# Where a running maximum's matmuls stand beside an attention tile's two score pairs, and where the matmuls of a key difference stand behind its values' matmul

## The chip, the cores and the metric

One NeuronCore of a Trainium2 chip runs the whole program, in one launch. The metric is the device time of one execution in microseconds. Of the kernel before three executions were timed; a fourth was taken with the hardware profiler.

## The reference

Four transformer layers work on x, 1024 tokens by 128. In each, x is increased by a cross-attention over 6404 context rows (16 heads of 8), and then by a mixture of 8 experts of which each token uses 2. Layers 0, 1 and 3 use a softmax, layer 2 a sigmoid. Cut to what matters here:

```
for l in 0..3:
    q = split_heads(norm(x) @ Wq.T + bq)         # 16 heads, 1024 x 8 each
    k, v = split_heads(ctx @ Wk.T + bk), split_heads(ctx @ Wv.T + bv)   # 6404 x 8 each
    s = q @ k.T / sqrt(8)                         # 16 x 1024 x 6404
    a = softmax(s) if l != 2 else sigmoid(s)
    x = x + (a @ v, heads joined) @ Wo.T + bo
    x = x + experts_l(norm(x))                    # top 2 of 8, gated (l = 2: gelu)
```

The softmax needs, for each query and head, a number near the largest score, so that no exponential overflows. The change concerns when those largest scores are found.

## The kernel before, in words

**Tiles and phases.** Tokens are taken in two blocks of 512 queries, so layer and block give 8 units; heads are taken in groups of 4, so there are 32 phases (4 per unit; `phase`, L122). A phase goes over 51 tiles of 128 keys. A tile has two score pairs: pair 0 is heads 0 and 1 of the group, pair 1 heads 2 and 3. Each pair is two matmuls of 32 x 128 against 32 x 512 in f16 (L787) into one half of the PSUM tensor `scores`, and one exponential of 128 x 1024 on ScalarE (L956). The four heads stand on four groups of 32 rows of TensorE: heads 0 and 1 ("half 0") on rows 0 to 63, heads 2 and 3 ("half 1") on rows 64 to 127. The values' matmul `av` (L797, eight matmul records of fp32) for the tile before follows behind pair 1.

**Maxima.** While phase p runs, the maxima of phase p+1 are prepared: 176 matmuls per phase (L818), each 128 queries of one head against 512 keys, into one of three banks of the PSUM tensor `side`; VectorE reduces each (L1070). 144 are plain. For the first 2048 keys a saving is made: two chunks are combined, since max(a, b) = b + relu(a - b). The stacks of differences of keys lie in `K` beside the keys; a `dif` step (L809) multiplies a pair of heads by such a difference into a half of `scores`, ScalarE takes the relu into the SBUF tile `above` (L964), and two combined maxima (L1074) add the second chunk's scores to it and reduce. There are 16 differences and 32 combined maxima per phase. `above` is single: a relu waits for both combined maxima of the difference before it.

**Waits.** `scores` has two halves, used in turn by score pairs, differences and some of the feed-forward matmuls (`in_pairs`, L166): a user waits until the one two before it has been read. `side` has three banks, used by maxima, transposes, `oT`, `flipmax`, routing and `down` (the experts' second matmul, L913; it holds its bank from its first chunk to the read of its sum). `Order.__init__` (L187) gives each user the bank that came free longest ago, and `bank_free` (L762) makes TensorE wait for the last reader of it. TensorE takes its steps strictly in the order of the list.

**The planner.** `attention_steps` (L427) writes the order of all steps by hand. Time there is counted in quarters of a tile, `t`. In quarter 0 come score pair 0 and its exponential and then maxima of half 1, in quarter 2 score pair 1 and maxima of half 0, in quarter 3 `av` of the tile before, one maximum of the half of which more are left (at a tie half 1), and a difference if one is due and both combined maxima of the last one are out. Background work (the last unit's feed-forward network, the next layer's keys and values, loads) is put in at its due time at the end of each quarter; its matmuls fall in quarter 1, between the two pairs (`placed`, L388). `find(half, t, most)` (L469) puts out up to `most` maxima of a half, and stops as soon as the planned VectorE time spent reaches the share of the window that has passed (`spent`, `total`, planned costs in `COST`: 0.62 for a plain maximum, 0.7 for a combined one). A phase's window begins 12 quarters before the phase ahead of it and ends 12 quarters before the phase itself; in its last 8 quarters `find` may take 5.

The program also has a path for masked inputs, which these inputs (a mask of ones) don't take.

Of the kernel before, what the change touches and what calls it, by code (L numbers as in the profile page):

```python
# [89 lines left out]
def both_of(d):  # L90

    qt, half, i = DIFS[d]
    return [ITEMS.index((qt, 2 * i + 1, 2 * half + j)) for j in range(2)]
# [19 lines left out]
def softmax(l):  # L113
    return l != 2


def unit(u):

    return u // 2, u % 2


def phase(p):  # L122

    return p // 8, p // NG % 2, p % NG
# [235 lines left out]
def finish_steps(u):  # L360

    l, b = unit(u)
    out = []
    if u >= 0:
        if softmax(l):
            out += [(0, Step("POOL", "bvadd", (u,))), (0, Step("POOL", "boadd", (u,)))]
        out += [(8, Step("PE", "oflip", (u,))), (1, Step("ACT", "oflipc", (u,))), (4, Step("PE", "oproj", (u,))),
                (3, Step("DVE", "resid", (u,)))]
        out += norm_steps(u, "f")
        if l == 1:  # L370
            out.append((0, Step("POOL", "zcopy", (u,))))
        for lp in range(FFN[l]["loops"]):
            if l == 1:
                out += norm_steps(u, f"r{lp}")
            out += flip_steps(u, f"r{lp}" if l == 1 else "f")
            out += pass_steps(u, lp)
        if l == 1:
            out.append((1, Step("POOL", "zadd", (u,))))
    if l < 3:
        out += norm_steps(u, "a") + flip_steps(u, "a")  # L380
        for g in range(NG):
            out += [(1, Step("PE", "qproj", (u, g))), (0, Step("ACT", "qsplit", (u, g))), (0, Step("POOL", "qadd", (u, g)))]
    else:
        out.append((2, Step("SP", "out", (b,))))
    return out


def placed(at, steps, taken):  # L388


    out = []
    for gap, s in steps:
        at += gap
        if s is not None and s.eng == "PE":
            at += (1 - at) % 4
            while at in taken:
                at += 4
            taken.add(at)
        if s is not None:
            out.append((at, s))  # L400
    return out


def loads(u):

    l, b = unit(u)
    out = []
    if b:
        if l + 2 < 4:
            out += [(2, Step("SP", "wattn", (l + 2,))), (0, Step("DVE", "bqs", (l + 2,)))]  # L410
        if l + 1 < 4:
            out.append((0, Step("SP", "wo", (l + 1,))))
        out.append((0, Step("SP", "wffn", (l,))))
        if l == 3:
            out.append((0, Step("DVE", "b1s", (l,))))
    return out
# [10 lines left out]
def attention_steps(units):  # L427

    first, last = NG * units[0], NG * units[-1] + NG - 1
    back = []  # L430
    taken = set()
    for p in range(first, last + 1):
        at = p * Q
        if p + 1 < 32 and softmax(phase(p + 1)[0]):
            back += [(at + Q - LEAD - 1, Step("DVE", "fina", (p + 1,))), (at + Q - LEAD - 1, Step("DVE", "finb", (p + 1,))),
                     (at + Q - 7, Step("PE", "flipmax", (p + 1,))), (at + Q - 5, Step("DVE", "finc", (p + 1,)))]
            taken.add(at + Q - 7)
        if p > first:
            back += [(at + 3, Step("ACT", "drain", (p - 1,))), (at + 13, Step("PE", "oT", (p - 1,)))]
            if softmax(phase(p - 1)[0]):  # L440
                back.append((at + 15, Step("DVE", "rden", (p - 1,))))
            back.append((at + 15, Step("DVE", "norm", (p - 1,))))
            taken.add(at + 13)
        if p + 2 < 32:
            back.append((at + Q - LEAD - 4 if softmax(phase(p + 2)[0]) else at + 2 * Q - 8, Step("POOL", "fill", (p + 2,))))
            back += [(at + 4 * e + 2, Step("SP", "kload", (p + 2, i))) for i, (a, e) in enumerate(K_PIECES)]
            back += [(at + 6, Step("SP", "kload", (p + 2, len(K_PIECES) + i))) for i in range(NDIF)]
    for u in units:
        at = NG * u * Q
        if u:  # L450
            back += placed(at + 16, finish_steps(u - 1), taken)
    for u in units:
        l, b = unit(u)
        at = NG * u * Q
        back += placed(at + 2, loads(u), taken)
        if b == 0 and l < 3:
            back += placed(at + 24, kv_steps(l + 1), taken)
    back.sort(key=lambda x: x[0])

    def window(p):  # L460

        return max(first * Q, (p - 1) * Q - LEAD), p * Q - LEAD

    out = []
    n = 0
    p = first + 1
    spent, single, both, ready, ahead, total = 0.0, [], [], [], [], None

    def find(half, t, most):  # L469

        nonlocal spent
        a, e = window(p)
        for _ in range(most):
            if t < e - 8 and spent >= total * (t + 1 - a) / (e - 8 - a):
                return
            if both[half] and (ready[half][0] <= t if ready[half] else False):
                i = both[half].pop(0)
                if both_of(ITEM_DIF[i])[1] == i:
                    ready[half].pop(0)
                spent += COST["both"]  # L480
            elif single[half]:
                i = single[half].pop(0)
                spent += COST["red"]
            else:
                return
            out.append(Step("PE", "max", (p, i)))
            out.append(Step("DVE", "red", (p, i)))

    for t in range(first * Q, (last + 1) * Q):
        kt, q = t // 4 % KT, t % 4  # L490
        if t >= window(p)[1]:
            assert total is None or not (single[0] or single[1] or both[0] or both[1] or ahead)
            p, total = p + 1, None
        has = p <= last + 1 and p < 32 and softmax(phase(p)[0]) and t >= window(p)[0]
        if has and total is None:
            a, e = window(p)
            half_of = len(HALVES[0])
            spent, single = 0.0, [list(range(0, half_of)), list(range(half_of, FIRST_BOTH))]
            both = [[i for i in range(FIRST_BOTH, len(ITEMS)) if ITEMS[i][2] // 2 == half] for half in range(2)]
            ready = [[], []]  # L500
            ahead = [(a + (e - 24 - a) * d // len(DIFS), d) for d in range(len(DIFS))]
            total = FIRST_BOTH * COST["red"] + (len(ITEMS) - FIRST_BOTH) * COST["both"]
            total += sum(COST.get(s.what, 0.15) for at, s in back if s.eng == "DVE" and a <= at < e - 8)
        if q in (0, 2):
            half = q // 2
            out.append(Step("PE", "score", (t // Q, kt, half)))
            out.append(Step("ACT", "exp", (t // Q, kt, half)))
            if has:
                find(1 - half, t, 2 if t < window(p)[1] - 8 else 5)
        if q == 3:  # L510
            if kt:
                out.append(Step("PE", "av", (t // Q, kt - 1)))
            elif t // Q > first:
                out.append(Step("PE", "av", (t // Q - 1, KT - 1)))
            if has:
                find(0 if len(single[0] + both[0]) > len(single[1] + both[1]) else 1, t, 1)
            if has and ahead and ahead[0][0] <= t and not ready[0] and not ready[1]:
                d = ahead.pop(0)[1]
                out.append(Step("PE", "dif", (p, d)))
                out.append(Step("ACT", "relu", (p, d)))  # L520
                ready[DIFS[d][1]].append(t + 5)
        while n < len(back) and back[n][0] <= t:
            s = back[n][1]
            out.append(s)
            if s.eng == "DVE":
                spent += COST.get(s.what, 0.15)
            n += 1
    out.append(Step("PE", "av", (last, KT - 1)))
    out.append(Step("ACT", "drain", (last,)))
    out += [Step("PE", "oT", (last,))] + [Step("DVE", "rden", (last,))] * softmax(phase(last)[0]) + [Step("DVE", "norm", (last,))]  # L530
    out += [s for at, s in back[n:]]
    return out
# [80 lines left out]
def build(nc, A, out):  # L613
    ctx = ExitStack()
    with ctx:
# [1141 lines left out]
        with nc.Else():  # L1757
# [4 lines left out]
            run([s for s in layer0 if s.what in ("kv", "kc", "vc", "ksplit", "kput", "ctx") or s.what in in_attention  # L1762
                 and s.key[0] >= 8 and s.what not in ("score", "exp", "av")])
        run(attention_steps(range(2, 8)))
        run(plain(finish_steps(7)))

# [71 lines left out]
```

## Time and profile before

| | us |
|---|---|
| median of 3 timed runs | 4637.65 |
| lowest and highest | 4628.42, 4646.2 |
| the profiled execution | 4653.02 |
| its span, first to last instruction | 4651.2 |

The span is one execution taken by the profiler; 1.8 us of the profiled time lie around it. TensorE's busy time is that of matmuls whose ends are modelled, so neighbouring matmuls can overlap in it. PEld is TensorE's weight load, which runs beside matmuls. A wait "A <- B" is idle time of an engine before A that ended when B did. ScalarE's instructions of 1.02 us follow each other at about 0.92 us. The numbers of the phases can be told from the drain of the values' bank at each phase's start; phase 3 runs from 594.4 to 718.0 us, phase 9 from 1433.8 to 1591.5, phase 25 from 3607.5 to 3788.8 and phase 31 from 4468.0 to 4564.9.

### The profile page before, as it was taken

The numbers are of one execution on the slowest core, as the hardware profiler recorded it, in microseconds if no ns is written. First come the engines' busy times: TensorE is split into PE (matmuls) and PEld (weight loads), VectorE is DVE, ScalarE is ACT, GpSimd is POOL, SyncE is SP. The second block draws the span as 40 slices with busy tenths as digits, with TensorE's granted clock in tenths as the row PEclk, the third lists the DMA queues.
The fourth block names the chain that finished last, engine by engine and source line by source line (L and its number), as shares of the span: only waits on it lengthen the run. The fifth ranks groups of instructions, "written<-read, shape, count | busy, mean of one in ns | idle before, by whom it ended". The sixth has DMA issues, their size and how long they took to land. (4 is left out here: it accounts for less than half of the span.)

```text
span 4651.2 us, 69670 instructions
## 1 busy us (share of the span) xinstructions
PE 3977.9 (86%) x26742; PEld 905.9 (19%) x26742; DVE 2817.9 (61%) x5645; ACT 3939.7 (85%) x4355; POOL 830.5 (18%) x719
## 2 busy tenths in 40 slices
PE   6888888888789888888989999888888888888887
PEld 2121111111122211122212222111111111122112
DVE  4878888778777788867501110110486668876833
ACT  3589998899888889888898889978988888888994
POOL 4010001520025200352412111111000210035002
PEclk7699999999999999999999999999999999999998
DMA  4221001100011100111102121110001100010001
GB/s 123 63 63 30 12 14 32 34 12 13 15 52 35 44 24 19 32 32 35 32 17 70 44 68 31 34 39 17 15 12 37 35 11 12 12 38 27 9 1 48
DMA packets 124358, 150.38 MB, mean 32 GB/s; under 512 B 29208, under 2 KB 76320, under 8 KB 124016
## 3 DMA queue, kind: packets, MB, share of 16 engines
q1 hardware_dynamic: 122576, 145.05, 11.6%
q8 instruction: 212, 3.47, 0.3%
q14 instruction: 130, 1.06, 0.1%
q10 hardware_dynamic: 1440, 0.79, 0.1%
HBM read 122.24 MB, written 23.51 MB: 31 GB/s over the span
## 5 line engine op out<-in xcount | busy, mean ns | idle before, releaser
L956 ACT ACTIVATE prob<-scores 128x1024 f32<-128x1024 f32 x3264 | 3177.7, 1025 | 314.2 <-PE scores L787 299.6
L1070 DVE TENSOR_REDUCE mpart<-side 128x1 f32<-128x512 f32 (+1 forms) x3456 | 2124.2, 657 | 729.8 <-PE side L818 719.1
L797 PE MATMUL av<-prob,VA 128*9 128x512 f32 x6528 | 875.0, 609 | 1.7 <-ACT prob L956 0.8
L797 PE MATMUL av<-prob,VB 128*9 128x512 f32 x6528 | 874.0, 608 | 1.3 <-ACT prob L956 0.5
L787 PE MATMUL scores<-QP,KA 32*128 32x512 f16 x3264 | 641.9, 395 | 195.1 <-ACT above L964 118.3
L787 PE MATMUL scores<-QP,KB 32*128 32x512 f16 x3264 | 631.3, 388 | 191.3 <-ACT above L964 93.7
L818 PE MATMUL side<-KA,QP 32*128 32x512 f16 (+1 forms) x2112 | 625.1, 392 | 39.6 <-DVE mpart L1070 20.7
L818 PE MATMUL side<-KB,QP 32*128 32x512 f16 (+1 forms) x2112 | 584.8, 386 | 43.2 <-DVE mpart L1070 29.2
L1074 DVE CUSTOM_DVE_ANT_0 above<-side,above 128x512 f32<-128x512 f32 x768 | 514.0, 686 | 76.0 <-PE side L818 70.0
L964 ACT ACTIVATE above<-scores 128x1024 f32<-128x1024 f32 x384 | 393.5, 1025 | 178.9 <-PE scores L809 116.1
L787 PEld LDWEIGHTS scores<-QP,KB 32*128 32x128 f16 x3264 | 151.8, 91 | 867.7 <-ACT prob L956 537.1
L787 PEld LDWEIGHTS scores<-QP,KA 32*128 32x128 f16 x3264 | 151.3, 91 | 821.0 <-ACT prob L956 442.5
L818 PEld LDWEIGHTS side<-KA,QP 32*128 32x128 f16 x2112 | 147.5, 91 | 601.5 <-DVE mpart L1070 450.0
L818 PEld LDWEIGHTS side<-KB,QP 32*128 32x128 f16 x2112 | 140.0, 91 | 593.4 <-DVE mpart L1070 453.8
L895 PE MATMUL scores<-xnT,Fin 128*128 128x512 f32 (+1 forms) x256 | 146.1, 653 | 44.4 <-ACT above L964 31.7
L913 PE MATMUL side<-hT,Fout 128*128 128x512 f32 (+1 forms) x304 | 172.5, 654 | 8.0 <-POOL hT L1373 4.2
L1290 POOL TENSOR_TENSOR o_tok<-o_tok,bvo 128x512 f32<-128x512 f32 x6 | 7.6, 1270 | 886.9 <-DVE o_tok L1111 487.2
L1351 POOL TENSOR_TENSOR ag<-ag 128x512 f32<-128x512 f32 (+1 forms) x80 | 101.7, 1271 | 329.7 <-ACT ag L1015 329.7
L797 PEld LDWEIGHTS av<-prob,VA 128*9 128x9 f32 x6528 | 97.0, 88 | 194.8 <-issue 187.2
L797 PEld LDWEIGHTS av<-prob,VB 128*9 128x9 f32 x6528 | 97.0, 88 | 192.6 <-issue 185.1
L1400 POOL CAST hi<-kb 128x512 f16<-128x512 f32 (+1 forms) x60 | 35.9, 598 | 549.0 <-ACT kb L1045 546.7
L1101 DVE RECIPROCAL rden<-side 128x16 f32<-128x16 f32 x24 | 6.0, 250 | 209.6 <-PE side L836 209.6
(185 smaller groups left out, 2541.5 us busy)
## 6 DMA issues: line engine op xcount, KB each, us to landing
cwb<-weights SPq DMA_DIRECT2D x80, 256.0 KB, 3.8
KA<-kstacks SPq DMA_DIRECT2D x384, 48.0 KB
KB<-kstacks SPq DMA_DIRECT2D x384, 48.0 KB
Fin<-in_Fin SPq DMA_DIRECT2D x64, 256.0 KB, 2.8
kstacks<-hi SPq DMA_DIRECT2D x112, 128.0 KB, 2.4
ctxc<-in_ctxT SPq DMA_DIRECT2D x48, 256.0 KB, 3.0
kstacks<-lo SPq DMA_DIRECT2D x56, 128.0 KB, 2.6
hT<-in_mask SPq DMA_DIRECT2D x16, 400.2 KB, 3.4
```

Source lines behind the costliest of these rows:

```text
L787: last = pe.matmul(pair[:, j, :], K[p % 2][rows(h), kt * P:kt * P + P], QP[p % 3][rows(h), :], start=True, stop=True)
L797: last = pe.matmul(AV[ROWS * h:ROWS * h + VC, :], V[l % 2][:, kt, g * HG + h, :], prob[:, (e + h // 2) % RING, (h % 2) * QB:(h % 2) * QB + ...
L818: pe.matmul(bank[:, 0:chunk_of(c)], QP[p % 3][rows(h), qt * P:(qt + 1) * P], K[p % 2][rows(h), chunk(c)], start=True, stop=True).then_inc( ...
L895: pe.matmul(bank[0:fs, :], Fin[:, w, j * fs:(j + 1) * fs], x[:], start=True, stop=True).then_inc(sem["bgP"], 1)
L913: pe.matmul(bank, Fout[0:fs, w, c, :], h, start=first, stop=c == nk - 1).then_inc(sem["bgP"], 1)
L956: act.activation(prob[:, e % RING, :], pair.rearrange("p a b -> p (a b)"), ACT.Exp if softmax(l) else ACT.Sigmoid, scale=SCALE).then_inc(s ...
L964: act.activation(above[:].rearrange("p a b -> p (a b)"), pair.rearrange("p a b -> p (a b)"), ACT.Relu).then_inc(sem["bgA"], 1)
L1070: dve.tensor_reduce(part, bank, AX.X, ALU.max).then_inc(sem["red"], 1)
L1074: dve.tensor_tensor_reduce(more, bank, more, 1.0, LEAST, ALU.add, ALU.max, part).then_inc(sem["red"], 1)
L1290: pool.tensor_tensor(o_tok[:], o_tok[:], broadcast(bvo[l % 2][:, 0, :].unsqueeze(1), full), ALU.add).then_inc(sem["bgG"], 1)
L1351: pool.tensor_tensor(a, a, g, ALU.mult).then_inc(sem["bgG"], 1)
L1400: pool.tensor_copy(hi16[:, slot, 0:w], k).then_inc(sem["bgG"], 1)
```

## The change

Behind score pair 0 (half = 0) the cap stays 2, behind score pair 1 (half = 1) it is 1 instead of 2; in the last 8 quarters of a window both stay 5. In quarter 3 the difference now comes directly behind `av`, and the one maximum behind it. Since `ready` and the left-over lists are changed by `find`, whether a difference is due is now asked before that maximum is chosen. The opening (`opening_steps`), which prepares the maxima of phase 0, isn't touched.

```diff
@@ attention_steps
             out.append(Step("PE", "score", (t // Q, kt, half)))
             out.append(Step("ACT", "exp", (t // Q, kt, half)))
             if has:
-                find(1 - half, t, 2 if t < window(p)[1] - 8 else 5)
+                find(1 - half, t, 2 - half if t < window(p)[1] - 8 else 5)
         if q == 3:
             if kt:
                 out.append(Step("PE", "av", (t // Q, kt - 1)))
             elif t // Q > first:
                 out.append(Step("PE", "av", (t // Q - 1, KT - 1)))
-            if has:
-                find(0 if len(single[0] + both[0]) > len(single[1] + both[1]) else 1, t, 1)
             if has and ahead and ahead[0][0] <= t and not ready[0] and not ready[1]:
                 d = ahead.pop(0)[1]
                 out.append(Step("PE", "dif", (p, d)))
                 out.append(Step("ACT", "relu", (p, d)))
                 ready[DIFS[d][1]].append(t + 5)
+            if has:
+                find(0 if len(single[0] + both[0]) > len(single[1] + both[1]) else 1, t, 1)
```

## Rows read from the trace of the kernel before

**Rows 1.** The page: busy us of each engine (share of the span) xinstructions.
```profile
PE 3977.9 (86%) x26742; PEld 905.9 (19%) x26742; DVE 2817.9 (61%) x5645; ACT 3939.7 (85%) x4355; POOL 830.5 (18%) x719
```

**Rows 2.** Groups: out<-in xcount | busy us, mean ns | idle before, releaser.
```profile
L956 ACT ACTIVATE prob<-scores 128x1024 f32<-128x1024 f32 x3264 | 3177.7, 1025 | 314.2 <-PE scores L787 299.6
L1070 DVE TENSOR_REDUCE mpart<-side 128x1 f32<-128x512 f32 (+1 forms) x3456 | 2124.2, 657 | 729.8 <-PE side L818 719.1
L964 ACT ACTIVATE above<-scores 128x1024 f32<-128x1024 f32 x384 | 393.5, 1025 | 178.9 <-PE scores L809 116.1
```

**Rows 3.** Stretches, phases 3, 31, 9: stretch, length, busy us (xinstructions), clock, DMA, GB/s.
```profile
594.40:718.00 123.60, 100.82 (x829) 20.05 (x829) 108.25 (x217) 112.34 (x120) 0.00 (x0) 1.00 0.05 13
4468.00:4564.90 96.90, 87.03 (x622) 16.07 (x622) 0.55 (x2) 95.47 (x105) 0.00 (x0) 1.00 0.00 1
1433.80:1591.50 157.70, 139.87 (x935) 33.65 (x935) 111.98 (x216) 139.92 (x167) 63.24 (x54) 1.00 0.12 33
```

**Rows 4.** Waits: first 200 to 2300, then the whole span (us, times, longest).
```profile
ACT prob L956 <- PE scores L787: 83.0, 179, 6.5
...
ACT above L964 <- PE scores L809: 116.1, 210, 2.2
ACT above L964 <- DVE mpart L1074: 44.8, 46, 2.9
...
ACT above L964 <- DVE mpart L1070: 12.8, 26, 1.0
```

**Rows 5.** Timeline, 504.3 to 507.6: start, us, engine, line, op, out<-in xcount [idle].
```profile
504.40 0.39 PE L818 MATMUL side<-KB,QP 32*128 32x512 f16 x1
504.40 0.39 PE L787 MATMUL scores<-QP,KA 32*128 32x512 f16 x2
...
505.02 0.39 PE L787 MATMUL scores<-QP,KA 32*128 32x512 f16 x2 [0.23 <-ACT prob L956]
...
505.58 0.38 PE L818 MATMUL side<-KB,QP 32*128 32x512 f16 x1 [0.16 <-DVE mpart L1074]
...
506.87 0.39 PE L809 MATMUL scores<-KB,QP 32*128 32x512 f16 x2
...
507.33 1.02 ACT L964 ACTIVATE above<-scores 128x1024 f32<-128x1024 f32 x1 [0.53 <-DVE mpart L1070]
```

**Rows 6.** Timeline around 1400 (two maxima ahead of down) and around 1463 (one).
```profile
1399.44 0.38 PE L818 MATMUL side<-KB,QP 32*128 32x512 f16 x1
...
1400.28 0.39 PE L818 MATMUL side<-KB,QP 32*128 32x512 f16 x1 [0.45 <-DVE mpart L1070]
...
1400.66 1.02 ACT L956 ACTIVATE prob<-scores 128x1024 f32<-128x1024 f32 x1
...
1403.59 1.02 ACT L956 ACTIVATE prob<-scores 128x1024 f32<-128x1024 f32 x1 [0.32 <-PE scores L787]
...
1462.96 1.02 ACT L956 ACTIVATE prob<-scores 128x1024 f32<-128x1024 f32 x1
...
1464.35 1.96 ACT L956 ACTIVATE prob<-scores 128x1024 f32<-128x1024 f32 x2
```

**Rows 7.** Idle time of TensorE and its weight load before L913 (us, times).
```profile
  DVE mpart L1070: 8.0, 24
```

**Rows 8.** Timeline, 1546.6 to 1547.9: a half-0 maximum ahead of pair 0.
```profile
1546.75 0.38 PE L818 MATMUL side<-KA,QP 32*128 32x512 f16 x1
...
1546.98 0.62 PE L787 MATMUL scores<-QP,KB 32*128 32x512 f16 x3
...
1547.39 1.02 ACT L956 ACTIVATE prob<-scores 128x1024 f32<-128x1024 f32 x1 [0.23 <-PE scores L787]
```

**Rows 9.** Timeline, 510.2 to 512.3: a difference of half 1 behind a half-1 maximum.
```profile
511.55 0.59 PE L809 MATMUL scores<-KB,QP 32*128 32x512 f16 x2
```

**Rows 10.** Stretch and group, 100 to 200 us, the lower clock.
```profile
100.00:200.00 100.00, 89.57 (x208) 16.29 (x209) 89.92 (x182) 41.13 (x48) 0.00 (x0) 0.50 0.31 86
L818 PE MATMUL side<-KA,QP 32*128 32x512 f16 (+1 forms) x141 | 79.9, 579 | 5.3 <-DVE mpart L1074 4.2 <-DVE mpart L1070 0.8
```

## The prediction

> **What bounds the kernel now.** The page gives no single bound: TensorE is busy 86% of the span and ScalarE 85%, VectorE 61% [rows 1]. The groups say what fills them: 3264 exponentials (L956) and 384 relus (L964) of 1.02 us on ScalarE, and 3456 plain maxima of 0.66 us (and 768 combined ones) on VectorE [rows 2]. VectorE's 61% is an average over phases with maxima and phases without. So I read two stretches next. Phase 31, which prepares no maxima, takes 96.9 us with ScalarE busy 95.5; phase 3, quiet but for maxima, takes 123.6 us with ScalarE busy 112.3 and VectorE 108.3 [rows 3]. In the 23 phases with maxima both are close to full, and what ScalarE loses it loses in short waits. These are for TensorE: 83.0 us before exponentials from 200 to 2300 us, the stretch with 15 of those 23 phases, and over the whole span 116.1 us (210 times) before relus, with 44.8 + 12.8 us more (72 times) put down to VectorE [rows 4].
>
> The timeline shows how such a wait arises [rows 5]. `side` has three banks. In this tile the score pair goes at 505.02, but the second maximum beside it finds its bank taken and goes at 505.58. TensorE works in order, so the values' matmul waits behind it; the next maximum and the difference go at 506.87, and the relu starts at 507.33, 0.53 us after ScalarE was free. What stands in TensorE's queue ahead of the next score pair decides.
>
> **What the change does to the order.** The planner allows maxima by a budget: 144 x 0.62 + 32 x 0.7 = 111.7 planned us (more with background work) over 196 quarters of a tile, 0.57 per quarter, so some 3.7 maxima per tile. One quarter lies before the first score pair, two before the second, one before the values' matmul: today's order is mostly 1 + 2 + 1. With the cap of 1 beside the second pair the arrears pass to the next place that may take two, and the order becomes mostly 2 + 1 + 1. No maximum is removed: 176 per phase stay, against room for 4 x 49. Two things follow. Half 1 (heads 2, 3) is served twice beside the first pair, half 0 once beside the second, so more of half 0 is left and the maximum behind the values' matmul, today nearly always half 1, becomes half 0 (I take 85%; ties give half 1). And all three side banks are asked for at once, ahead of whatever the planner puts between the two pairs.
>
> **Part 1: the fourth maximum, no term.** Whether the maxima go 1 + 2 or 2 + 1, the one directly ahead of the values' matmul is the fourth since the last, and needs the bank of the first, which VectorE frees about 1.17 us after that one started (504.40 to 505.58) [rows 5]. In quiet tiles its wait stays. I cost the plain move at 0; a tile with 3 maxima waits in neither kernel.
>
> **Part 2: a background matmul behind two maxima, +54 us.** A down matmul (L913) holds a side bank over its two to four steps. With one maximum ahead of it a bank is free. With two, either the second maximum or the down matmul waits for VectorE, and the second score pair stands behind both. The trace has one such tile: the first maximum is issued at 1399.44, the second at 1400.28 (0.84 us later, with a wait for VectorE), and the down matmul and the second score pair stand behind it; the tile lasts 1400.66 to 1403.59, 2.93 us. A like tile with one maximum ahead of its down matmul starts at 1462.96 and lasts about 2.3 us (the two exponentials from 1464.35 end 1.96 us later, so the second, the next tile's, starts 1.02 us before that end, at 1465.3) [rows 6]. So a tile costs between 0.6 and 0.84 us; I take 0.7, between the tile's length and the single wait. The order holds 110 down steps between pairs in the phases with maxima (experts x chunks: 16 for units 0, 1 and 6, 32 for units 2 and 5, less two behind the last pairs). The budget gives two maxima in about 0.7 of them (3.7 - 2 = 1.7 on average). 110 x 0.7 x 0.7 = 54 us; bounds 0 (if pacing gives one there) and 110 x 0.84 = 92. Today these matmuls wait only 8.0 us on VectorE, in 24 waits [rows 7].
>
> **Part 3: other users of a side bank between the pairs, +10 us.** oT and flipmax (44) stand right behind a relu tile, where ScalarE has a microsecond of cover; transposes, logits and projections (38) often don't. If a third of the 38 costs 0.7 us, that is 9; with a little for the rest I take 10. Bounds 0 and 82 x 0.7 x 0.6 = 34.
>
> **Part 4: a maximum of half 0 ahead of the first pair, +37 us.** Two matmuls on different 32-row groups start together: at 504.40 a half-1 maximum and both score matmuls. Today's few exceptions show the other case: a half-0 maximum at 1546.75, the second score matmul only at 1546.98, and the exponential at 1547.39 [rows 8]. From maximum to ScalarE that is 0.64 us, against 506.87 to 507.33 = 0.46 us when the groups differ [rows 5]: 0.18 us. Places: 33 tiles per phase end without a difference, 759 in all. Some 275 of them hold other matmuls; there TensorE and ScalarE take turns and I charge three quarters: 275 x 0.85 x 0.18 x 0.75 = 31 us. In quiet tiles (some 385 of the rest) it would be 59 us, but there the chain maximum, VectorE, values' matmul, difference sets when the relu starts, and the maximum itself isn't late: ScalarE just waits that much less at the relu. I take a tenth, 6. Bounds 0 and 100.
>
> **Part 5: the difference directly behind the values' matmul, -25 us.** It no longer queues behind a maximum. Where both are of one half that costs today: the difference's two matmuls take 0.59 us at 511.55, against 0.39 at 506.87 [rows 5, 9]. Half of the differences are of half 1, as the maximum is; (210 + 72) / 2 = 141 relus that waited, x 0.18 = 25 us [rows 4]. The maximum goes later instead, and what is behind it, the next first pair, waits for the relu's exponential anyway: 0. No DMA is moved, and no queue of SP or POOL is passed.
>
> **Part 6: relus that wait for a combined maximum just issued, -14 us.** A relu overwrites `above` and so waits for both combined maxima of the last difference: 44.8 us in 46 waits, 0.97 each, against 116.1 / 210 = 0.55 for the ordinary one [rows 4]. With the difference ahead of the maximum, one that was just due makes the difference wait for the next tile, and the relu waits the ordinary time: 46 x 0.42 = 19 us, less the opening's share, which isn't changed: 14. Bounds 0 and 19.
>
> **Sum.** 54 + 10 + 31 + 6 - 25 - 14 = +62 us against the profiled execution, which took 4653.0 us for a span of 4651.2. That execution is 15.4 us above the median of the three runs, and I put the difference on the median: 4637.65 + 62 = 4700 us, 1.3% slower. The case's own range, with the terms' bounds not all on one side, is +25 to +140.
>
> **Rivals.** *Faster: the wait beside the second pair goes.* If the one maximum left there found a bank, because VectorE gets its work 0.55 us earlier and is further on, the 0.53 us before the relus and half of the exponentials' waits go: about 116 x 0.6 + 83 x 23 / 15 x 0.25 = 100 us, with parts 5 and 6 mostly inside it, so 4540 us. It speaks for it that VectorE is idle 15 us in phase 3 [rows 3]; against it, that VectorE's first free bank depends on the maximum behind the values' matmul, which doesn't move. It decides from the point where fewer than half of the tiles with a difference show the wait. Chance 0.13 that this, wholly or in part, outweighs the rest; in part it ends near 4600.
>
> *No change: the banks' cover holds.* If the budget mostly leaves one maximum beside the first pair in tiles with a down matmul, or the cost falls on tiles where ScalarE had slack, part 2 falls to 20 and part 4 to 15: 20 + 5 + 15 - 39 = 0, 4638 us. Chance 0.16. That the edit hardly alters the order belongs here.
>
> *Slower by the clock.* In phase 3, full of waits for banks, the granted clock is 1.00, the 2.4 GHz level [rows 3]; at 0.50 a maximum's matmul takes 0.58 us instead of 0.39 [rows 5, 10]. Were the clock halved in the down tiles, 110 x 2.7 us of TensorE work would double: about 4930 us. Chance 0.02. The Trainium skill ("TensorE: Matmul & The Clock Gate", section "A second HAM failure mode: psum-queue depth-cycling") says that short idle gaps from cycling through PSUM banks can make the clock swing between its levels; by that rule the new waits would cost far more than their length. This case's trace disagrees so far, with 1.00 in the stretch named.
>
> **Chances.** Forecast 0.69, no change 0.16, faster 0.13, clock 0.02. So slower by over 0.5% (23 us, about what a measurement of this kernel can tell) 0.71, within 0.5% 0.16, faster 0.13. The range runs from the no-change case, with a little below it, to the forecast's upper end: 4630 to 4780.
>
> **What would show it.** Down matmuls waiting for VectorE (L1070, L1074) in many more than 24 waits and some 50 us; exponentials (L956) waiting clearly more for scores in phases 4 to 14 and 24 to 29, less or the same in phases 2, 3, 6, 11; relus waiting less than today's 174 us, with the 44.8 us for L1074 nearly gone. Phases 15 to 22 and 31 must not change. I am wrong if phase 3 falls well below 123.6 us (then the fourth maximum's wait went) or if phase 9 stays at 157.7 us [rows 3].

## The result and the profile after

| | before | after |
|---|---|---|
| first comparison, medians (4 and 3 runs), us | 4639.5 | 4692.93 |
| ratio, 95% interval | | 1.0139 [1.0107, 1.0172] |
| the changed kernel taken again, medians, us | 4644.41 (22 runs) | 4683.56 |
| ratio, 95% interval | | 1.0076 [1.0059, 1.0093] |
| span of the profiled execution, us | 4651.2 | 4681.2 |

The change makes the kernel slower, by 0.8% (39 us) in the comparison with more runs and by 1.4% in the first. The intervals don't overlap: the first holds a run of 4745.61 us at a mean granted clock of 0.918, where the others stood at 0.962 and 0.967 (a fourth, at 0.64, is left out). I take the second, 35 us by its ratio and 39 by its medians, as the size; the parts below are measured against it.

The clock hides a part of the loss. In the second comparison the kernel before ran at a mean granted clock of 0.956 (4662.45 us) to 0.964 (4632.66 us), and its 22 times fall by about 3.4 us for each 0.001 of clock. The changed kernel ran at 0.964 to 0.968 (4690.81 to 4677.44 us, the same slope). At 0.964 it took 4690.81 us, and the four executions of the kernel before at 0.964 took 4632.66 to 4636.17. So at the same clock the change costs some 55 us (an estimate from these times), and a higher clock took some 16 of them back. Why its clock is higher, no run here shows.

The page's line of engines, and its groups for exponentials and relus, of the kernel after:

```profile
PE 4082.3 (87%) x26742; PEld 937.1 (20%) x26742; DVE 2816.9 (60%) x5645; ACT 3947.0 (84%) x4355; POOL 829.7 (18%) x719
...
L956 ACT ACTIVATE prob<-scores 128x1024 f32<-128x1024 f32 x3264 | 3191.3, 1025 | 414.3 <-PE scores L787 402.9
...
L964 ACT ACTIVATE above<-scores 128x1024 f32<-128x1024 f32 x384 | 393.8, 1026 | 87.7 <-PE scores L809 64.1
```

The work is the same [rows 1, 2]. The idle time has moved: 100 us more before exponentials (314.2 to 414.3), 91 us less before relus (178.9 to 87.7), and 13 us more before the copy of a down matmul's result (L1031, 10.0 to 23.1, shown with the experiments). The waits of the kernel after, over the whole span, and the idle time of TensorE before L913, show the same from the releasers' side:

```profile
ACT prob L956 <- PE scores L787: 402.9, 839, 37.0
...
ACT above L964 <- PE scores L809: 64.1, 183, 1.3
...
ACT above L964 <- DVE mpart L1074: 18.0, 21, 2.0
```
```profile
  DVE mpart L1070: 40.6, 56
```

The waits of relus for L1070 are gone, those for L1074 fell from 44.8 to 18.0, and the down matmuls wait 40.6 us for a bank where they waited 8.0 [rows 4, 7].

The stretches of phases 3, 31, 9, 25 and 0 of the kernel after (stretch, length, busy us of PE, PEld, DVE, ACT, POOL, clock, DMA, GB/s):

```profile
586.50:709.00 122.50, 107.45 (x827) 22.40 (x826) 107.64 (x214) 112.56 (x120) 0.00 (x0) 1.00 0.05 13
4498.10:4595.10 97.00, 87.08 (x622) 16.09 (x622) 0.55 (x2) 95.60 (x104) 0.00 (x0) 1.00 0.00 1
1424.70:1587.10 162.40, 145.02 (x938) 34.23 (x937) 112.95 (x218) 141.06 (x166) 63.20 (x54) 1.00 0.12 32
3607.20:3810.30 203.10, 165.37 (x916) 35.51 (x915) 111.76 (x214) 149.03 (x155) 39.32 (x22) 0.89 0.09 23
189.80:331.50 141.70, 124.09 (x913) 31.88 (x910) 114.25 (x222) 124.47 (x137) 22.00 (x25) 0.98 0.21 55
```

Phase 25 of the kernel before:

```profile
3607.50:3788.80 181.30, 152.57 (x916) 34.91 (x916) 111.68 (x215) 148.49 (x156) 39.35 (x22) 0.92 0.10 26
```

Phase 31 stands, quiet phase 3 became 1.1 us shorter, phase 9 4.7 us longer [rows 3], and phase 25 went from 181.3 to 203.1. So the loss lies where the feed-forward work runs, and the quiet phases give a little back. Phase 25 alone, with 26 of the 110 down tiles, makes 21.8 us; phases 5, 9, 13, 24, 28 and 29 make 4.6 to 7.7 us each; phase 0 went from 149.0 us at a clock of 0.94 to 141.7 at 0.98. TensorE's clock in phases 3 and 9 is 1.00 as before.

A tile of phase 9 with a down matmul in the kernel after (timeline):

```profile
1430.88 0.39 PE L818 MATMUL side<-KA,QP 32*128 32x512 f16 x1
...
1431.51 1.02 ACT L956 ACTIVATE prob<-scores 128x1024 f32<-128x1024 f32 x1 [0.48 <-PE scores L787]
...
1432.04 0.39 PE L818 MATMUL side<-KA,QP 32*128 32x512 f16 x1 [0.57 <-DVE mpart L1070]
...
1432.36 1.13 PE L913 MATMUL side<-hT,Fout 96*128 96x512 f32 x2
...
1433.41 0.39 PE L787 MATMUL scores<-QP,KB 32*128 32x512 f16 x2
...
1433.52 0.60 ACT L1031 ACTIVATE yb<-side 128x512 f32<-128x512 f32 x1 [0.99 <-PE side L913]
...
1434.01 1.02 ACT L956 ACTIVATE prob<-scores 128x1024 f32<-128x1024 f32 x1
```

The second maximum waits for its bank until 1432.04; the down matmul and the second score pair stand behind it, and ScalarE, free at 1432.53, has nothing for 0.99 us: part 2 of the prediction in one tile.

### The profile page after: what moved, and what is told of

Read it like the earlier page. It is cut to its first block and busy times, and to the rows that moved or that the text cites. A ratio compares the mean times of both kernels' runs of the same rounds, so it can differ in the third digit from the quotient of the medians.

```text
span 4681.2 us, 69644 instructions
## 1 busy us (share of the span) xinstructions
PE 4082.3 (87%) x26742; PEld 937.1 (20%) x26742; DVE 2816.9 (60%) x5645; ACT 3947.0 (84%) x4355; POOL 829.7 (18%) x719
## 5 line engine op out<-in xcount | busy, mean ns | idle before, releaser
L956 ACT ACTIVATE prob<-scores 128x1024 f32<-128x1024 f32 x3264 | 3191.3, 1025 | 414.3 <-PE scores L787 402.9
L1070 DVE TENSOR_REDUCE mpart<-side 128x1 f32<-128x512 f32 (+1 forms) x3456 | 2125.0, 656 | 763.2 <-PE side L818 747.5
L797 PE MATMUL av<-prob,VB 128*9 128x512 f32 x6528 | 863.6, 601 | 1.4 <-ACT prob L956 0.5
L787 PE MATMUL scores<-QP,KA 32*128 32x512 f16 x3264 | 696.6, 388 | 139.2 <-ACT above L964 71.8
L787 PE MATMUL scores<-QP,KB 32*128 32x512 f16 x3264 | 685.9, 387 | 147.4 <-ACT prob L956 69.8
L818 PE MATMUL side<-KA,QP 32*128 32x512 f16 (+1 forms) x2112 | 612.0, 391 | 54.7 <-DVE mpart L1070 40.3
L818 PE MATMUL side<-KB,QP 32*128 32x512 f16 (+1 forms) x2112 | 564.3, 377 | 47.8 <-DVE mpart L1070 36.2
L1074 DVE CUSTOM_DVE_ANT_0 above<-side,above 128x512 f32<-128x512 f32 x768 | 513.3, 685 | 75.7 <-PE side L818 71.3
L964 ACT ACTIVATE above<-scores 128x1024 f32<-128x1024 f32 x384 | 393.8, 1026 | 87.7 <-PE scores L809 64.1
L913 PE MATMUL side<-hT,Fout 128*128 128x512 f32 (+1 forms) x304 | 173.8, 658 | 22.3 <-DVE mpart L1070 13.8
```

What stands on the lines that cost most here:

```text
L787: last = pe.matmul(pair[:, j, :], K[p % 2][rows(h), kt * P:kt * P + P], QP[p % 3][rows(h), :], start=True, stop=True)
L797: last = pe.matmul(AV[ROWS * h:ROWS * h + VC, :], V[l % 2][:, kt, g * HG + h, :], prob[:, (e + h // 2) % RING, (h % 2) * QB:(h % 2) * QB + ...
L818: pe.matmul(bank[:, 0:chunk_of(c)], QP[p % 3][rows(h), qt * P:(qt + 1) * P], K[p % 2][rows(h), chunk(c)], start=True, stop=True).then_inc( ...
L913: pe.matmul(bank, Fout[0:fs, w, c, :], h, start=first, stop=c == nk - 1).then_inc(sem["bgP"], 1)
L956: act.activation(prob[:, e % RING, :], pair.rearrange("p a b -> p (a b)"), ACT.Exp if softmax(l) else ACT.Sigmoid, scale=SCALE).then_inc(s ...
L964: act.activation(above[:].rearrange("p a b -> p (a b)"), pair.rearrange("p a b -> p (a b)"), ACT.Relu).then_inc(sem["bgA"], 1)
```

## The experiments

Each ratio is that of the timed runs to the kernel before on the same chip (4644 to 4646 us in all three sittings). "Cap a/b" is what `find` may put out beside pair 0 and beside pair 1. Every edit is shown against the changed kernel.

**One part at a time.** e1 has the new cap and the old place of the difference:

```diff
+            if has:
+                find(0 if len(single[0] + both[0]) > len(single[1] + both[1]) else 1, t, 1)
             if has and ahead and ahead[0][0] <= t and not ready[0] and not ready[1]:
@@
-            if has:
-                find(0 if len(single[0] + both[0]) > len(single[1] + both[1]) else 1, t, 1)
```

> Only the cap behind the second score pair goes from 2 to 1; the difference stays behind the quarter's maximum. Theory (the cap costs through side banks and shared row groups, the moved difference gives back about 39 us): slower than the kernel with both edits, +95 us against the kernel before, ratio 1.015 to 1.025, with the down matmuls' waits for VectorE as in the kernel after (40 to 50 us) and the relus' waits back above 120 us. Rival (the moved difference is what costs): ratio under 1.01.

e2 has the old cap (2/2) and the new place of the difference:

```diff
-                find(1 - half, t, 2 - half if t < window(p)[1] - 8 else 5)
+                find(1 - half, t, 2 if t < window(p)[1] - 8 else 5)
```

> Only the difference moves directly behind the values' matmul; the cap stays 2. Theory: faster than before by about 39 us, ratio 0.990 to 0.995, relus' waits down from 174 us to about 130, waits put down to the combined maxima nearly gone outside the opening, exponentials' waits unchanged. Rival (the difference's place is worth nothing, relus just wait elsewhere): 0.998 to 1.002.

Measured: e1 1.0313 [1.0295, 1.0331], e2 0.9924 [0.9908, 0.9941]. The two halves of the change pull apart: the difference's move gains 35 us, the cap alone loses 145, and together they lose 35. So they don't add: under the new cap the move is worth 110 us. A part of the reason is in the waits of e1:

```profile
ACT above L964 <- DVE mpart L1074: 76.5, 84, 2.2
```

With half 0 behind the values' matmul, the combined maximum put there directly ahead of the difference is one that the relu must wait for, 84 times where the kernel before had 46 [rows 4]. With both edits these waits are 18.0 us in 21, and all waits of relus in the phases with maxima fall from 137 us in e1 to 76. That is 61 of the 110 us. The other half goes with the clock, as far as these runs tell: e1 ran at 0.944 to 0.952, the changed kernel at 0.964 to 0.968, and this run doesn't tell the cause. Brought to 0.964 by 3.4 us per 0.001, the cap alone costs about 106 us, the difference's move gains 24, and both together cost 55 (estimates), so the gap between the sum and the whole is smaller than it looks, but stays. e1 lies above the 1.015 to 1.025 expected of it; e2 is as expected, but its waits for L1074 aren't nearly gone (37.1 us).

**The cap, in three classes of tiles.** e3, e5 and the changed kernel itself allow three maxima beside the two pairs together, and differ only in the tiles in which two of them may go ahead of the second pair. (e2 allows 2/2, and its order is mostly 1 + 2 + 1.) e3 has one ahead in the tiles whose background matmul uses a `side` bank, 2/1 in the others:

```diff
+    crowded = {at // 4 for at, s in back if s.eng == "PE" and s.what in SIDE and not in_pairs(s.what, s.key)}
@@
-                find(1 - half, t, 2 - half if t < window(p)[1] - 8 else 5)
+                find(1 - half, t, (1 + half if t // 4 in crowded else 2 - half) if t < window(p)[1] - 8 else 5)
```

> The kernel after, but in tiles with a background matmul on a side bank between the pairs the caps are 1 and 2 as before. Theory: the cap's cost in down tiles goes (54 + 10 us predicted), ratio to before about 1.003 (0.998 to 1.008); the down matmuls wait for VectorE about 8 us again; phases 5, 9, 13, 24, 25, 28, 29 lose most of what they gained in length. Rival (slower through the row groups or through the clock alone): stays at 1.010 or above.

e5 has one ahead in every tile with a background matmul:

```diff
+    filled = {at // 4 for at, s in back if s.eng == "PE" and True}
@@
-                find(1 - half, t, 2 - half if t < window(p)[1] - 8 else 5)
+                find(1 - half, t, (1 + half if t // 4 in filled else 2 - half) if t < window(p)[1] - 8 else 5)
```

> The difference directly behind the values' matmul; caps 1 and 2 in every tile that holds a background matmul, 2 and 1 in the others. Theory (the cap costs only where a background matmul stands between the pairs, and in quiet tiles VectorE's chain covers the shared row group): as fast as the difference alone or 5 to 15 us faster, ratio 0.989 to 0.993, phases 5, 9, 24, 29 as long as in the kernel before. Rival (the cap costs in quiet tiles too): 0.996 or more.

The changed kernel unaltered, in the same sitting as e5:

> The changed kernel itself, beside the kernel before on the chip of the other three. Theory and rival alike: ratio 1.010 to 1.017. If the waits for side banks and row groups are the cause, its spread stays within 1% and its granted clock is no lower than that of the kernel before; if a lower clock is the cause, its runs spread with the clock and it has the lower one.

It came out below its expected range, at a clock that was higher than the other's, and not lower. e5 fell between its theory and its rival.

| | two ahead of pair 1 in | ratio [95%] | step, us |
|---|---|---|---|
| e2 | none | 0.9924 [0.9908, 0.9941] | -35 |
| e5 | quiet tiles | 0.9947 [0.9928, 0.9967] | +11 |
| e3 | quiet tiles and those with a user of `scores` | 0.9989 [0.9978, 1.0001] | +19 |
| changed kernel | all | 1.0076 [1.0059, 1.0093] | +40 |

A step is the difference of two ratios times 4645 us, so that their sum is the whole by construction; what the table shows is which class of tiles each part belongs to. Each step is uncertain by some 10 us. With every time brought to a clock of 0.964 as above, the steps would be +8, +26 and +45 us (estimates). The largest belongs to the side banks. In e3 TensorE's idle time before the down matmul (L914 there) is

```profile
  DVE mpart L1071: 2.7, 5
```

against 40.6 us in 56 waits. Read tile by tile from the traces, the down tiles in the phases with maxima:

| down tiles | number | mean wait of exponential 0, 1 | all of ScalarE's waits from exponential 0 to 1 |
|---|---|---|---|
| before, one maximum ahead, not behind a relu | 64 | 0.26, 0.28 | 0.69 |
| after, two ahead, not behind a relu | 49 | 0.45, 0.65 | 1.53, +0.84 each |
| before, one ahead, behind a tile with a relu | 26 | 0.00, 0.03 | 0.03 |
| after, two ahead, behind a tile with a relu | 23 | 0.00, 0.37 | 0.45, +0.42 each |

The last column holds more than the exponentials, because ScalarE also waits to copy the down matmul's result (L1031), before and after:

```profile
ACT yb L1031 <- PE side L913: 10.0, 23, 0.5
```
```profile
ACT yb L1031 <- PE side L913: 23.1, 28, 1.2
```

49 x 0.84 + 23 x 0.42 = 51 us of waits. Some of it is won back before the next tile: from its first exponential to that of the next tile, the 110 down tiles last 355.5 us in all before, as much in e3, and 400.5 after. These 45 us are the third step. A relu's microsecond on ScalarE covers part of it in a third of the tiles.

The second step, e5 to e3, was meant to be the shared 32-row group (part 4) in tiles with an `up` or another user of `scores`; that it is, isn't shown. ScalarE's waits, read tile by tile, grow by 11 us in these tiles (97.1 to 107.7) and by 10 in the tiles with another user of a side bank than down (24.2 to 33.9), which have one maximum ahead in both kernels. The same edit also puts a second maximum ahead of `up`. Phase 9 of e5:

```profile
1423.88:1580.18 156.30, 141.17 (x935) 34.12 (x935) 112.20 (x216) 139.52 (x167) 63.08 (x54) 1.00 0.13 33
```

It is 156.3 there, 161.9 in e3, 162.4 after: in this phase, and in phase 5 (150.8, 155.4, 156.3), nearly all of the loss comes with the second step and little with the third, whose 40 us lie in phases 25 (12.8) and 29 (8.4) above all. Two score pairs with a maximum ahead, first one of e2 (other rows), then one of the kernel after (the same rows), both timelines of phase 9:

```profile
1438.70 0.39 PE L818 MATMUL side<-KA,QP 32*128 32x512 f16 x1
1438.70 0.39 PE L787 MATMUL scores<-QP,KB 32*128 32x512 f16 x2
...
1439.16 1.02 ACT L956 ACTIVATE prob<-scores 128x1024 f32<-128x1024 f32 x1 [0.16 <-PE scores L787]
```
```profile
1451.06 0.38 PE L818 MATMUL side<-KA,QP 32*128 32x512 f16 x1
...
1451.07 0.39 PE L787 MATMUL scores<-QP,KB 32*128 32x512 f16 x1
...
1451.29 0.37 PE L787 MATMUL scores<-QP,KB 32*128 32x512 f16 x1
...
1451.71 1.02 ACT L956 ACTIVATE prob<-scores 128x1024 f32<-128x1024 f32 x1 [0.34 <-PE scores L787]
```

From the maximum to the exponential it is 0.46 us in the one and 0.65 in the other.

**Two ahead in down tiles alone.** e6 puts the cap 2/1 into the tiles with a side bank's user and leaves 2/2 elsewhere:

```diff
-                find(1 - half, t, 2 - half if t < window(p)[1] - 8 else 5)
+                find(1 - half, t, (2 - half if t // 4 in crowded else 2) if t < window(p)[1] - 8 else 5)
```

> The difference directly behind the values' matmul and caps as before, but 2 and 1 in tiles with a side-bank user between the pairs. By the order 30 down tiles (of 110) then have two maxima ahead of the down matmul. Theory: 0.6 to 0.85 us for each, 20 to 25 us, and some 10 us for half-0 maxima behind the values' matmul: ratio 0.998 to 1.002, the down matmuls' waits for VectorE up by 10 to 20 us. Rival (the banks' wait is covered): as the difference alone, 0.992.

Measured: 0.9984 [0.9969, 1.0000], 28 us above e2 for 30 down tiles. The profiled span grew by 35 us, of which 9.6 are phase 0, at a clock of 0.88 instead of 0.98. The down tiles show 19 us: ScalarE's waits from exponential 0 to 1 are 1.39 us in 25 of the 30 and 0.27 in the 5 behind a relu, against 0.69 and 0.03 in e2's tiles with one maximum ahead. They lie before the copy of the down result (L1032 there; 26.0 us in 31 waits, e2 8.5 in 24) and not before the exponentials. It agrees with the table in size.

**Two ahead in tiles with a user of `scores` alone.** e7 and e9, with `filled` now the tiles for which `in_pairs` holds:

```diff
e7:  find(1 - half, t, (1 + half if t // 4 in crowded else 2 - half if t // 4 in filled else 2) if t < window(p)[1] - 8 else 5)
e9:  find(1 - half, t, (2 - half if t // 4 in filled else 2) if t < window(p)[1] - 8 else 5)
```

> The difference directly behind the values' matmul and caps as before, but 2 and 1 in tiles whose background matmul uses a half of the scores (up, keys and values, queries); by the order no down tile has two ahead, and 124 maxima of half 0 stand behind the values' matmul in tiles with background work. Theory: no bank wait, only the shared row group, 124 x 0.18 x 3/4 = 17 us: ratio 0.995 to 0.997. Rival (the row group is covered there too): 0.992. Rival (any second maximum between the pairs costs, bank or not): 1.000 or more.

> The kernel with the difference moved alone (0.992), plus the cap 2 - half in tiles whose background matmul takes a half of scores (103 such tiles with two maxima ahead of the second pair instead of 2, and 124 half-0 maxima ahead of a pair 0 there instead of 6). Unlike in e7, tiles with users of a side bank keep their caps. Theory of the shared rows alone: 118 x 0.18 x 0.75 = 16 us, ratio 0.996. Rival, two maxima ahead of the second pair cost as much here as in tiles with a down matmul (0.3 to 0.4 us or more each): 16 + 35, ratio 1.003, as e7 gave; then phases 5 and 9 stand at 156 and 162. If it is about 0.996, e7's rest came from its forced single maximum in the tiles with a side bank's user.

Measured: e7 1.0031 [1.0019, 1.0044], e9 1.0046 [1.0030, 1.0063]: 50 and 57 us above e2, three times what the shared rows alone should cost, although e5 to e3 had given 19 for the same class. Phases 5 and 9 of e9 are 152.2 and 159.9 us, neither e2's (149.4, 156.5) nor the rival's 156 and 162. The mixed caps did something else: a tile held back to 2/1 leaves arrears, and the next, allowed 2/2, takes 2 + 2 + 1. There are 64 such tiles in e9, 50 in e6, 5 in e2 and none in the changed kernel. One of them in phase 10 of e9 (timeline; lines are one higher there):

```profile
1665.74 0.38 PE L819 MATMUL side<-KB,QP 32*128 32x512 f16 x1 [0.36 <-DVE mpart L1075]
...
1666.34 0.39 PE L819 MATMUL side<-KB,QP 32*128 32x512 f16 x1 [0.22 <-DVE mpart L1071]
...
1668.07 1.02 ACT L965 ACTIVATE above<-scores 128x1024 f32<-128x1024 f32 x1 [1.10 <-PE scores L810]
```

Two maxima in a row wait for banks, and the relu comes 1.10 us late. The 13 quiet relus of e9 with four maxima ahead of the difference wait 0.89 us on average. The arrears also reach the down tiles, whose caps are e2's: 37 of the 110 have two maxima ahead of the down matmul in e9, 1 in e2. From e2 to e9 ScalarE's waits grow by 21 us in down tiles (67.6 to 88.5), by 28 in quiet ones (15 of them in phase 0, at a clock of 0.89 against 0.98), by 4 in those of the other users of a side bank, and by only 11 in the tiles with a user of `scores`, which the experiment was about. In e7 the down tiles stand (66.1), the quiet ones give 32 and those with a user of `scores` 18. How these 11 and 18 us divide between the rows and the second maximum isn't settled.

**Keeping the shared rows off pair 0.** In e4, in tiles without a difference, the maximum waits until the next tile's first pair has gone:

```diff
+            if has and not half and late:
+                find(0 if len(single[0] + both[0]) > len(single[1] + both[1]) else 1, t - 1, 1)
+            late = False
@@
-            if has:
+            if has and out[-1].what == "relu":
                 find(0 if len(single[0] + both[0]) > len(single[1] + both[1]) else 1, t, 1)
+            else:
+                late = has
```

> The kernel after, but in tiles without a difference the maximum that stood behind the values' matmul stands behind the next tile's first score pair, so that no half-0 maximum is ahead of that pair. Theory: 0.18 us saved in some 200 to 300 places, 30 to 45 us less than the kernel after, ratio to before 1.004 to 1.008, with the exponentials' waits down by about that. Rival (covered everywhere): no change from the kernel after, 1.012 to 1.016.

e8 gives each pair the maxima of its own half, so that the one behind the values' matmul is mostly half 1:

```diff
-                find(1 - half, t, 2 - half if t < window(p)[1] - 8 else 5)
+                find(half, t, 2 - half if t < window(p)[1] - 8 else 5)
```

> The changed kernel, but the maxima beside a score pair are those of the pair's own half: half 0 (two) beside pair 0, half 1 (one) beside pair 1, so that the one behind the values' matmul is mostly half 1 again, on other rows than the next tile's pair 0 (52 half-0 maxima there in tiles with background matmuls, 253 in the changed kernel). Price paid: a maximum directly behind its own pair shares the rows with it and starts 0.2 us later. Theory of the shared rows ahead of pair 0: phases 5 and 9 fall by 3 to 5 us from the changed kernel's 156 and 162, in all 15 to 30 us back in the tiles with background work; in the quiet phases the later start of VectorE takes back 1 to 2 us a phase. Net ratio to the kernel before 1.000 to 1.005 (changed kernel 1.0076). Rival, the two maxima between the pairs cost by themselves, whatever half stands ahead of pair 0: phases 5 and 9 stay at 156 and 162 and the ratio stays at 1.007 or rises.

Measured: e4 1.0230 [1.0211, 1.0250], e8 1.0478 [1.0442, 1.0514]. Both expectations failed, by 1.5% and 4%, and the rivals named with them too. Phase 3 of e8:

```profile
614.69:741.05 126.36, 109.94 (x827) 23.29 (x825) 107.71 (x213) 113.25 (x120) 0.00 (x0) 1.00 0.05 12
```

It is 126.4 us there, 124.9 in e4 and 122.5 after, at the same clock. A maximum behind a pair on its own rows starts 0.23 us after it. A tile of that phase of e8 (timeline):

```profile
641.77 0.39 PE L787 MATMUL scores<-QP,KB 32*128 32x512 f16 x2
642.00 0.38 PE L818 MATMUL side<-KA,QP 32*128 32x512 f16 x1
```

VectorE starts that much later, and the maxima that wait for its banks too; the 174 quiet relus of e8 with three maxima ahead of the difference wait 0.45 us on average, against 0.37 after. In e4 it was the count: with the maximum put behind the next pair 149 quiet relus again have four maxima ahead of their difference, and these wait 0.70 us. It also has three maxima ahead of 49 down matmuls, whose second exponential waits 0.85 us, so neither run tests the row group by itself. That it costs on either side of a pair, and ahead of it less in quiet tiles, where ScalarE only waits that much less at the relu, is argued from these rows. Where the rest of e8's 4% comes from isn't settled: in the phases with background work it loses far more (phase 9 168.9 us, phase 25 217.5 at a clock of 0.87). It ran at a mean clock of 0.944 to 0.957, and by 3.4 us per 0.001 that goes with some 60 of the 187 us by which it is slower than the changed kernel.

**The best version.** e10 is e2 with at most one maximum ahead of a side bank's user:

```diff
+                find(1 - half, t, (1 + half if t // 4 in crowded else 2) if t < window(p)[1] - 8 else 5)
```

> The kernel with the difference moved alone, but with at most one maximum ahead of a side bank's user and the second score pair (cap 1 + half there, 2 elsewhere; it differs from the former in a few places only: down tiles with two ahead 1 to 0, others 2 to 0). Theory: the order is all but the same, ratio 0.992 as for the former, within 0.002. If a few badly placed tiles carry the waits of down matmuls that are left there (10.1 us in 29 waits), up to 5 us less.

Measured: 4607.93 us, 0.9914 [0.9898, 0.9931]. e2 and e10 can't be told apart; both beat the kernel before and the changed one. The difference directly behind the values' matmul with two maxima still allowed beside pair 1 is the version to keep.

## Why the prediction was right, and which of its terms were not

The sign, the place of the loss and its main cause, the waits behind two maxima in down tiles, came as forecast; 62 us were forecast, 39 measured by the comparison with 22 runs, some 55 at the same clock. That the sum comes so near is in part luck: several terms are off, in both directions, and the clock isn't among them.

**Part 1 failed.** "In quiet tiles its wait stays", I wrote, because the maximum directly ahead of the values' matmul is the fourth since the last. But the same change takes one place for a maximum away beside pair 1 and puts the one behind the values' matmul behind the difference too. What counts for the relu is how many stand between pair 0 and the difference, and that fell from four to three or two. Mean wait of the relus in quiet tiles, by the maxima since pair 0 that stand ahead of the difference (from the traces, tile by tile):

| maxima ahead | before | after |
|---|---|---|
| 4 | 184 relus, 0.56 us | none |
| 3 | 46, 0.42 | 151, 0.37 |
| 2 | 7, 0.04 | 81, 0.01 |

The test "wrong if phase 3 falls well below 123.6 us" came out at 122.5, a small fall, since the exponentials there wait more instead (3.2 to 6.5 us) as the relus wait less (8.1 to 4.0). That exponentials would wait "less or the same" in phases 2, 3, 6 and 11 was wrong too. The rival *faster* had the mechanism in part: a third of these relus (81 of 234) found TensorE on time.

**Parts 2 and 3, 64 us forecast, 40 measured.** The count was right: 72 of 110 down tiles have two maxima ahead (65% against 0.7), and 57 of the 82 other users of a side bank. The price of 0.7 us in part 2 was near: the down tiles became 45 us longer, 0.62 us for each of the 72, where 54 us were forecast. I had it from one tile, and it isn't one price: 0.84 us of waits without a relu ahead, 0.42 with one. For oT and flipmax I had named the relu's cover, for the down matmuls I forgot it. The 10 us of part 3 don't show in the third step (the waits in these tiles are 33.9 us in e3 and 30.9 after), but against the kernel before they are up by 14 (16.6), as they are in e2 (32.5), which has the old cap; so they aren't the cap's alone. What is left of the difference to 64 us goes with the clock: brought to 0.964, the third step is 45 us.

**Part 4, 31 + 6 us forecast, 19 + 11 measured.** 83% of the maxima ahead of pair 0 are half 0 (I took 85%), and in the tile shown the exponential comes 0.19 us later (0.65 against 0.46). The 19 are the step in which tiles with a user of `scores` change; its cause isn't shown to be the rows. Part of the term for tiles with side bank users lies in the 40. That it is covered in quiet tiles holds: phase 3 is no longer than in e2 (123.4). The 11 us of the step to e5 don't lie there; its profiled execution loses them in phases 0 (146.3 us at a clock of 0.91 against 140.1 at 0.98), 8 and 28.

**Parts 5 and 6, -39 us forecast, -35 measured.** The sum is right and its division isn't: in e2 the relus wait 37 us less in the phases with maxima (166.8 to 130.2), but in the quiet ones only a few tenths of a microsecond each (phase 3 8.1 to 8.0); the gain comes in phases with background work, 2 to 5 us each, in some of them (4, 23, 26) at a clock higher by 0.02 to 0.03, and in phase 0, 8.9 us at 0.98 against 0.94. At the same mean clock e2 gains about 24 us (an estimate as above), so some 10 of the 35 may be the clock's. The waits for L1074 fell only from 44.8 to 37.1 in e2, since there half 1 stands behind the values' matmul; it is in the new cap's presence that the move saves the most (76.5 in e1, 18.0 after). I had priced the two edits one by one.

**The clock** was no rival in phases 3 and 9, at 1.00 after as before. It fell in phase 25, from 0.92 to 0.89, and to 0.87 in e8. In that phase, before as after, TensorE stops three times for some 6 us while ScalarE loads a table, works through two gelus (L1026) and loads the exponential's table again, and each stop is followed by a stretch at the lower level. Around the third stop, before and then after:

```profile
3740.00:3745.00 5.00, 0.14 (x1) 0.00 (x0) 1.26 (x3) 4.97 (x4) 3.06 (x3) 0.68 0.00 0
3745.00:3755.00 10.00, 8.11 (x35) 1.22 (x35) 4.56 (x7) 6.81 (x8) 6.33 (x3) 0.50 0.00 0
```
```profile
3755.00:3760.00 5.00, 0.57 (x7) 0.13 (x10) 0.00 (x0) 4.97 (x5) 4.68 (x3) 0.57 0.00 0
3760.00:3775.00 15.00, 14.00 (x53) 2.19 (x50) 7.25 (x13) 7.14 (x8) 4.58 (x2) 0.50 0.00 1
```

Over the phase TensorE is at 0.50 for 27 us before and 44 after. In phase 0 of the changed kernel (last section) 20 us more at 0.50 went with 6.3 us of time, so these 17 would make about 5 of the phase's 21.8 us (an estimate); ScalarE's waits before exponentials and relus in its down tiles grow by 13.6. The Trainium skill ("TensorE: Matmul & The Clock Gate", section "A second HAM failure mode: psum-queue depth-cycling") would have such waits swing the clock. Phases 3 and 9, with the same kind of waits at 1.00, speak against it; phase 25 and e8 could be read for it; no run here separates the two causes.

## What to carry to other kernels

When several users rotate over few banks and the engine in front works strictly in order, count how many ask for a bank ahead of the instruction that feeds the bottleneck, and in which tiles: the same reordering gained in quiet tiles and lost in those where a long holder of a bank came third. Price two edits of one schedule together, each in the order that the other leaves, and let experiments divide the tiles as well as the edits. A cap that is right for one class of tiles moves its arrears into the next, so a mixed rule needs its own count, of the tiles too whose rule didn't change. And where executions of one kernel spread with the clock, compare two kernels at the same clock as well as by their medians.

## What the runs showed of the hardware

- The shared row group works both ways. That a maximum ahead of a pair on its rows delays the second score matmul was in the rows before [rows 8]; behind a pair it is the maximum that starts 0.23 us late (641.77 and 642.00 in e8). Phase 3 of e8, where the maxima stand so, was 3.9 us longer than the changed kernel's at the same clock; that the delay is the cause is argued.
- The clock of a stretch can differ between executions of one kernel. Phase 0 of the changed kernel took 141.7 us at 0.98 (above) and in its second profile, in the same code:

```profile
190.19:338.20 148.01, 130.47 (x912) 31.54 (x910) 114.24 (x222) 124.45 (x137) 22.02 (x25) 0.91 0.20 53
```

6 us of difference in one phase is a sixth of the effect studied; a phase that runs at less than full clock can't be compared from one profile each.
